# First route of a two-layer MoE block: rows turned by transposes and made by three engines in turn, the two experts of a token chosen batch by batch

## The reference, cut to what matters

```
h = _layernorm(x, axis=-1) * (1 + cb) + sb        # x: (4, 1024, 256); cb, sb: one row of 256 a batch
x = x + gb * _L0_ffn_ref(h, Wr, W1, W2, W3)

# in _L0_ffn_ref
xf = x.reshape(-1, C)                             # 4096 tokens of 256
gate_logits = xf @ Wr                             # 8 logits a token
w, idx = jax.lax.top_k(gate_logits, 2)            # the two best experts, the lower index where two are equal
w = jax.nn.softmax(w, axis=-1)
comb = jnp.sum(w[:, :, None] * jax.nn.one_hot(idx, NUM_EXPERTS), axis=1)
```

## Time and profile before

| what | value |
|---|---|
| median of 3 runs | 2876.08 us (2870.78 to 2876.3) |
| the profiled execution, its own time | 2874.07 us |
| its span in the profile | 2872.4 us |
| TensorE's mean granted clock in it | 0.935 of full speed |
| busy share: PE, DVE, ACT, POOL | 86%, 73%, 45%, 43% |

### The profile page before, as it was taken

One profiled execution on the slowest core, in us unless ns is written; L12 is line 12 of the kernel. 1 busy time (PEld: TensorE's weight loads), 2 busy tenths in 40 slices (PEclk: granted clock), 3 DMA queues, 4 the chain that ended last, 5 costly groups with the idle time before them and its releaser, 6 DMA issues.

```text
span 2872.4 us, 38064 instructions
## 1 busy us (share of the span) xinstructions
PE 2483.7 (86%) x12341; PEld 1788.6 (62%) x12342; DVE 2102.1 (73%) x4278; ACT 1296.7 (45%) x2564; POOL 1238.7 (43%) x532
## 2 busy tenths in 40 slices
PE   6677868768776759999699999999999999959998
PEld 4455545545555549999366666666666666747776
DVE  4999999999999756666666667766776667655554
ACT  4677677677675335554233324332433243311111
POOL 2799999999999226666100000020002000233344
PEclk8889989889987879999899999999999999969999
DMA  4645555555557254444400010001001000125554
GB/s 149 195 155 189 169 178 190 167 182 189 163 179 219 75 163 91 63 63 60 125 1 1 1 48 1 1 31 33 1 1 34 15 1 1 67 84 125 128 132 75
DMA packets 151375, 268.84 MB, mean 94 GB/s; under 512 B 18348, under 2 KB 107612, under 8 KB 150844
## 3 DMA queue, kind: packets, MB, share of 16 engines
q1 hardware_dynamic: 122460, 227.12, 25.1%
q0 software_dynamic: 28224, 37.78, 8.1%
q10 hardware_dynamic: 544, 2.10, 0.2%
HBM read 209.52 MB, written 57.43 MB: 93 GB/s over the span
## 4 chain that ended last, share of the span: by engine, by line
PE 45%; DVE 3%; issue 2%; ACT 1%; DMA 1%; POOL 0%; another core or an unknown queue 0%; SPq 0%; DVEq 0%; POOLq 0%
PE at_o_ps L2007 8%; PE at_s_ps L1983 8%; PE at_qk_ps L1965 6%; PE e_h_ps L1584 5%; PE e_y_ps L1595 5%; PE at_s_ps L2015 4%; PE at_pt_ps L1994 4%; PE at_qk_ps L1970 3%; PE at_s_ps L1965 1%; DVE at_small L2384 1%; PE e_x_ps L1573 1%; PE at_s_ps L1970 0%; ACT at_pt L2144 0%; PE at_qk_ps L1903 0%; ACT at_probs L2133 0%
## 5 line engine op out<-in xcount | busy, mean ns | idle before, releaser
L793 POOL TENSOR_TENSOR dbx<-u,b_all 128x2048 f32<-128x2048 f32 x128 | 578.8, 4536 | 71.3 <-DVE u L872 31.6
L1847 POOL DMA_INDIRECT slots<-at_r_rows,slot_of x64 | 64.5, 1008 | 1101.7 <-DVE slot_of L2300 1021.9
L676 ACT ACTIVATE da_ps<-delta,a_neg 128x512 f32<-128x512 f32 x512 | 347.9, 689 | 132.6 <-DVE hc L945 124.3
L2144 ACT COPY at_pt<-at_pt_ps 128x512 f32<-128x512 f32 (+3 forms) x384 | 171.6, 483 | 515.0 <-PE at_pt_ps L1994 508.8
L469 PE MATMUL y_ps<-ident,hc 128*128 128x128 f32 x1536 | 246.8, 306 | 81.9 <-DVE hc L945 81.3
L1983 PE MATMUL at_s_ps<-at_qk 128*128 128x512 f32 (+3 forms) x768 | 290.8, 488 | 0.0
L2007 PE MATMUL at_o_ps<-at_pt,at_v 128*128 128x512 f32 (+3 forms) x768 | 288.4, 487 | 0.0
L469 PEld LDWEIGHTS y_ps<-ident,hc 128*128 128x128 f32 x1536 | 201.6, 158 | 137.0 <-DVE hc L945 108.5
L2133 ACT ACTIVATE at_probs<-at_s_ps,at_small 128x128 f32<-128x128 f32 (+7 forms) x256 | 192.1, 751 | 169.8 <-DVE at_small L2386 166.6
L945 DVE TENSOR_TENSOR hc<-da_ps,c_all 128x512 f32<-128x512 f32 x384 | 256.9, 671 | 0.0
L935 DVE TENSOR_TENSOR_SCAN da_ps<-da_ps,state,dbx 128x512 f32<-128x512 f32 x192 | 242.9, 1274 | 4.5 <-ACT da_ps L676 3.6
(11 more groups left out here) (409 smaller groups left out, 5011.5 us busy)
## 6 DMA issues: line engine op xcount, KB each, us to landing
b_all<-bc_rows SPq DMA_DIRECT2D x128, 512.0 KB, 4.6
c_all<-bc_rows SPq DMA_DIRECT2D x128, 512.0 KB, 5.0
w_qkv<-L_ffn_w SPq DMA_DIRECT2D x32, 512.0 KB
slots<-zeros SPq DMA_DIRECT2D x40, 260.0 KB, 6.5
e_xs<-slots SPq DMA_DIRECT2D x16, 650.0 KB, 7.1
w<-L_ffn_W SPq DMA_DIRECT2D x24, 384.0 KB, 8.8
more<-zeros SPq DMA_DIRECT2D x16, 256.0 KB, 5.1
sums<-x SPq DMA_DIRECT2D x8, 512.0 KB, 7.0
```

The source lines that it names most:

```text
L676: nc.scalar.activation(da_ps[s % RING_DA][:], delta[:, c % 2, m, :], ACT.Exp, scale=sh.a_neg[:, m, n:n + 1]).then_inc(S["da_ready"], 1)
L793: nc.gpsimd.tensor_tensor(dbx[:, at % RING_DBX], pair, rows, ALU.mult).then_inc(S["dbx_ready"], 1)
```

## The change

The rows of a tile are made by three engines. Even tiles: DVE computes `half = (x - mean) * rstd` (a tensor_scalar). Odd tiles: ACT computes the same as `x * rstd + dif`, with `dif = -mean * rstd` made once by DVE. Then DVE multiplies by `mods1` (a tensor_tensor), and POOL adds `mods0` and writes the row (a tensor_tensor, 32 of them). The waits on `row_turned` and `rows_copied` go with POOL's step. On ACT one such `normalise` of the next group stands behind copy 1 and one behind copy 3 of each group. PE turns with `nc.tensor.transpose` in place of a matmul against the identity. The choice is made for each batch by itself, with the same 12 instructions on 64 numbers a partition: that of batch b-1 stands on DVE behind the rows of batch b, the last two behind all rows. `scale` of the last tile of a batch stands in the next batch's part, so behind the choice, save for the last batch. ACT no longer raises `score_ready`.

```diff
+            pool.wait_ge(sh.route_mods_in, 16)
+            for t in range(TILES):
+                b, j = t // TPB, t % TPB
+                pool.wait_ge(half_ready, t + 1)
+                pool.wait_ge(row_turned, t + 1)
+                if j % CT == 0:
+                    pool.wait_ge(rows_copied[j // CT], b * 16 + 1)
+                nc.gpsimd.tensor_tensor(row8[:, j, :], half[:, t % 4, :], sh.mods[:, 0, b, :], ALU.add).then_inc(row_ready, 1)
...
+            def normalise(t):
+                act.wait_ge(row_ready, t + 1)
+                nc.scalar.activation(half[:, t % 4, :], sh.x[:, t, :], ACT.Identity, bias=sh.dif[:, t:t + 1],
+                                     scale=sh.rstd[:, t:t + 1]).then_inc(odd_ready, 1)
+            act.wait_ge(norm_ready, 1)
+            for t in (1, 3):
+                normalise(t)
...
                     if g < GROUPS:
                         copy_turned(g * GT + i)
+                        if i % 2 and g < GROUPS - 1:
+                            normalise((g + 1) * GT + i)
...
-            act.wait_ge(logits_copied, B)
-            act.sem_inc(score_ready, 1)
...
-                    last = nc.tensor.matmul(turned[t % RT][:, k, :], row8[:, t % TPB, k * P:(k + 1) * P], sh.ident[:], start=True, stop=True)
+                    last = nc.tensor.transpose(turned[t % RT][:, k, :], row8[:, t % TPB, k * P:(k + 1) * P], sh.ident[:])
...
-            pe.wait_ge(masks_ready, 1)
+            pe.wait_ge(masks_ready, B)
...
-            norm_rows(nc, dve, sh, half, row8, half_ready, row_ready, row_free)
+            nc.vector.scalar_tensor_tensor(out=sh.dif[:], in0=sh.mean[:], scalar=-1.0, in1=sh.rstd[:],
+                                           op0=ALU.mult, op1=ALU.mult).then_inc(norm_ready, 1)
+            def normalise(t):
+                dve.wait_ge(row_ready, t + 1)
+                nc.vector.tensor_scalar(half[:, t % 4, :], sh.x[:, t, :], sh.mean[:, t:t + 1], sh.rstd[:, t:t + 1],
+                                        ALU.subtract, ALU.mult).then_inc(even_ready, 1)
+            def scale(t):
+                dve.wait_ge(odd_ready if t % 2 else even_ready, t // 2 + 1)
+                nc.vector.tensor_tensor(half[:, t % 4, :], half[:, t % 4, :], sh.mods[:, 1, t // TPB, :], ALU.mult).then_inc(half_ready, 1)
+            def halves(b):
+                for t in range(b * TPB, (b + 1) * TPB, 2):
+                    normalise(t)
+                    if t:
+                        scale(t - 1)
+                    scale(t)
+                if b == B - 1:
+                    scale(TILES - 1)
...
+            def choose(b):
+                at = slice(b * TPB, (b + 1) * TPB)
+                dve.wait_ge(logits_copied, b + 1)
+                ...
+            for b in range(B):
+                halves(b)
+                if b == 0:
+                    dve.wait_ge(consts_ready, 8)
+                else:
+                    choose(b - 1)
+            choose(B - 1)
+            dve.wait_ge(masks_ready, B)
```

More of the change, by code:

```diff
@@ L1047, in phase_route @@
         (gate_in, var_ready, std_ready, chain, half_ready, row_ready, row_turned, turn_copied, tall_done, tall_copied, logits_done,
-         logits_copied, consts_ready, score_ready, masks_ready, ranked, gap_ready, exp_ready, meta_ready, meta_stored, lane_hot, block_hot, block_set, second_set, map_done, map_copied, held_done,
+         logits_copied, consts_ready, norm_ready, even_ready, odd_ready, masks_ready, ranked, gap_ready, exp_ready, meta_ready, meta_stored, lane_hot, block_hot, block_set, second_set, map_done, map_copied, held_done,
          pool_chain) = (
             sem(n) for n in ("gate_in var_ready std_ready chain half_ready row_ready row_turned turn_copied tall_done tall_copied logits_done "
-                             "logits_copied consts_ready score_ready masks_ready ranked gap_ready exp_ready "
+                             "logits_copied consts_ready norm_ready even_ready odd_ready masks_ready ranked gap_ready exp_ready "
                              "meta_ready meta_stored lane_hot block_hot block_set second_set map_done map_copied held_done pool_chain").split())
@@ L1233, in _ @@
-            nc.vector.tensor_tensor(both[:], mask[:, 0], mask[:, 1], ALU.add).then_inc(masks_ready, 1)
+            nc.vector.scalar_tensor_tensor(out=sh.dif[:], in0=sh.mean[:], scalar=-1.0, in1=sh.rstd[:],
[4 more added lines that the diff above has]
+                                        ALU.subtract, ALU.mult).then_inc(even_ready, 1)
@@ new lines, in _ @@
+            over = lambda a: a.rearrange("p (t o) -> p t o", o=1).broadcast_to([P, TPB, NE])
+            def choose(b):
+                at = slice(b * TPB, (b + 1) * TPB)
+                dve.wait_ge(logits_copied, b + 1)
+                values, c = logits[:, at, :], cand[:, at, :]
+                for k in range(2):
+                    link(nc.vector.tensor_reduce(top[:, k, at], values, AX_X, ALU.max))
+                    link(nc.vector.tensor_tensor(c, values, over(top[:, k, at]), ALU.is_lt))
+                    link(nc.vector.scalar_tensor_tensor(out=c, in0=c, scalar=float(NE), in1=iota_e[:, at, :], op0=ALU.mult, op1=ALU.add))
+                    chosen = meta[:, at, 3] if k == 0 else idx[:, at]
+                    link(nc.vector.tensor_reduce(chosen, c, AX_X, ALU.min))
+                    link(nc.vector.tensor_tensor(mask[:, k, at, :], iota_e[:, at, :], over(chosen), ALU.is_equal))
+                    if k == 0:
+                        link(nc.vector.scalar_tensor_tensor(out=scores[:, at, :], in0=mask[:, 0, at, :], scalar=-3e38, in1=values, op0=ALU.mult, op1=ALU.add))
+                        values = scores[:, at, :]
+                nc.vector.tensor_tensor(both[:, at, :], mask[:, 0, at, :], mask[:, 1, at, :], ALU.add).then_inc(masks_ready, 1)
```

## The result

The changed kernel takes 2879.32 us, the median of 16 runs (2878.14 to 2882.89), against 2873.45 of the kernel before on the same chip (16 runs, 2870.78 to 2876.3). The ratio is 1.0019, with a 95% interval of 1.0012 to 1.0025: 5.5 us slower by the ratio, 5.9 by the medians. In the profiled executions the span grew from 2872.4 to 2878.7, but the Mamba phase ahead, which the change doesn't touch, was also 2.0 longer, and the phases behind, whose code is the same, about 2 shorter. So the phase is read by itself, from its first DVE instruction (line 95; 969.96 before, 971.95 after) to the end of the choice: 52.05 us before, 58.23 after.

The account below looks back on a forecast made before the run. A loop of waits over PE and ACT, 4.97 us a period, was taken to bound the phase; -1.2 + 4.6 + 0.7 + 1.6 - 2.4 = +3.3 us on the median of 2876.08 gives 2879.4, range 2872 to 2891.

Parts of the forecast that it names:

- one of its own signs of being wrong: On PE in the groups: the forecast is wrong if PEclk is 0.50 there.
- the period: PE and ACT loop: two shorter turns -0.60, normalise +0.50, so 4.97 becomes 4.87, 4.37 in the last group; -1.2 us.
- the clock: First product on PE: clock still at 0.50 after gapped turning, 3.4 long in place of 1.8; +1.6 us, bounds 0 and 3.2.
- the choice: On DVE: row 8b+7 waits behind choose(b-1), product at +7.2 not +4.87; 2.3 lost for b = 1 and 2, +4.6.
- the start: Rows 0 to 3 come 1.2 to 1.3 apart in place of 0.8; first product at about 979.2, +0.7 us.
- the tail: After the last product: the wait for logits stays 3.29, the last batch's choice is 3.0 in place of 5.46; -2.4 us.
- a rival with a chance of 0.17: PE's clock stays at 0.50 in the groups: 7.1 a period, +15.2, 2891.3 us; chance 0.17.
- Rows in step: DVE and POOL take turns: 2.47 a pair of tiles, 1.24 a row against the loop's 1.22; lead small, not gone.
- SP's queue: Weight loads start 13 to 14 us later; SP done at about 1054, DVE's last instruction at 1060.6, so hidden by 6 to 7.
- The POOL rival: POOL's add with its waits at 1.0, 2.9 a pair: rows set the pace at 5.8 a group; +9, 2885; chance 0.13.

Follow-up runs that it names:

- the new order: The changed kernel with ScalarE copying the product's result ahead of copy 1, so copy 1 and normalise leave the loop; 0.9996.
- the last version: Kernel before with first four tiles turned by matmuls, others by transposes, ScalarE copying the product first, choice by batch behind all rows; 2865.36 us, 0.9967.

## Why the prediction was right, and where it was not

The forecast was 2879.4 and within 0.2% as the likeliest; measured are 2879.32 and +5.5 us by the ratio against a predicted +3.3, at the very edge of that bound (by the medians, +5.9, just over it). That the two times agree to 0.1 us is luck: the forecast stood on a median of 3 runs, 2876.08, and with 16 runs the kernel before is at 2873.45. The direction came out, and the size within a factor of two. The account behind them did not, and one of its own signs of being wrong came true: PEclk was 0.50 for a part of six groups. Term by term, with the measured value in the stretch: the period -1.2 (-0.9), the clock +1.6 (+8.7), the choice +4.6 (+0.5), the start +0.7 (+0.3), the tail -2.4 (-2.5); predicted +3.3, measured together +6.1 of the stretch's +6.2. Two terms, off by +7 and -4, cancelled in part.

- **The period, -1.2.** Right as a price. At full clock the loop of transposes and normalise is 4.91 (6.54 less 1.63 of slow product, second period), predicted 4.87; the last period is 4.42, predicted 4.37. Transposes alone gave 4.42, normalise alone +0.49.
- **The clock, +1.6 for the first product.** This term is the one that was mis-sized. I took the slow clock for the first product alone, where it cost 1.34, and left the groups to a rival with a chance of 0.17. The products were longer than 1.88 by 1.34, 1.63, 1.56, 1.38, 1.09, 0.91, 0 and 0: 7.9 us; slow first turns in four periods add 0.8. The runs show the cause: halved turning holds the clock (periods of 4.42), ScalarE's instruction in the loop with matmuls holds it (5.46), both together lose it, in a kernel that has nothing else of the change. The rival was right in its mechanism and too dear (7.1 a period): the clock recovered in each product, or just behind it, so a period paid 1.2 to 1.6, not 2.2.
- **The choice in the stream, +4.6.** Right as a mechanism, hidden here. The row does wait behind the choice; in the open, at the full clock, it costs 1.6 (with matmuls, the slow turn taken off), 1.29 (6.75 against 5.46, the last tile scaled ahead) or 2.97 (6.86 against 3.89, in the loop with the new order), against 2.3 predicted. In the changed kernel the slow product runs meanwhile. The two periods were 6.64, of which 1.56 and 1.09 are the product's and 0.08 and 0.25 the slow turn's: only 0.1 and 0.4 remain above 4.91. And around five of the six such stalls of the three runs above the clock fell for the next product, which the working didn't have.
- **Rows in step.** Rows were dearer in the working than on the chip: 2.47 a pair by strict turn-taking, 1.93 measured, so 0.27 a row less. The turn-taking itself is there: the instruction that starts second is the longer one, the tensor_scalar 0.81 against 0.405, the tensor_tensor 0.94 against 0.42, POOL's add 0.84 against 0.71 to 0.77. But an instruction's recorded time overlaps the other engine's at its edges, by 0.25 where VectorE is first, so the full times don't add up. The Trainium skill's rule (SBUF — State Buffer, "Who interferes with whom") that a two-input instruction of VectorE and a reading one of GpSimd block each other fits all 8 tensor_tensors that started inside a POOL add. The instruction of the earlier trace rows has one input, so it bears on the tensor_scalar and not on this rule. The fear of late rows in general fell with the run of three engines' rows alone: there the periods are all alike.
- **The start, +0.7.** +0.3: POOL's first rows came closer together than I took it.
- **The tail, -2.4.** -2.5. The choice of the last batch took 3.04.
- **SP's queue.** (The prediction's 1060.6 adds 3.8 where its own sum says 3.3; nothing hangs on it.) The meta store was issued at 1043.5 (15.0 later than before, counted from each phase's start; predicted 13 to 14), SP waited 11.3 for it, and was done at about 1056 against DVE's last instruction at 1065.3. Hidden, as predicted, by 9 us.
- **The Trainium skill's rule on transposes** (TensorE: Matmul & The Clock Gate, "Part 4: PE-mode transpose"), by which the full clock doesn't engage for them, isn't what happened: with every tile turned twice by transposes the clock was 1.00 from the first product to the last, also where the same loop with half as many let it fall (in the groups, products of 1.88 against up to 3.50).
- **Two sums of the prediction.** The POOL rival's terms, 3.3 and 6.6, give +9.9, not +9: the 1.2 was taken off though it is counted already. And its chances of a slower kernel, 0.17, 0.13 and a sixth of 0.58, add up to 0.40, not 0.33.

What stays open: which of the gaps within a group decides over the clock, and why it holds in one group and falls in another of the same kernel (it held at the third product of the run with ScalarE's extra instruction, and at the first of the two equal stalls of the run with the last tile scaled ahead). The runs change the amount of work (each tile turned twice) or the length of the loop (ScalarE's instruction); no run moved the same work about within a period. And the whole kernel gained 10.6 us by the medians with the last version (9.5 by the ratio) where its stretch gained 11.1; the rest is within the interval.

## What to carry to other kernels

An instruction handed to an idle engine is free only if it doesn't stand in the queue ahead of one that a loop waits for: ScalarE was busy for 2 of every 5 us before, yet 0.5 us of its time in the loop of waits cost 0.5 us each time, and the order of two of its instructions was worth 0.63 a period (4.42 to 3.79), where the transposes were worth 0.55 (4.97 to 4.42). Work taken off TensorE shortens its part of the loop, but the same loop with less work and more waiting may lose the clock, so shorten the wait first and the work after. And work cut in pieces belongs where its engine has nothing left to do: in the stream of rows the pieces gave back 1.0 of their 2.4 us with a spare lead of rows, and 3.2 and more without one; behind the rows they held nobody up.

## What the runs showed of the hardware that was not expected

Useless work can keep the clock: with ScalarE's extra instruction in the loop, twice as many transposes kept the granted clock at 1.00 (2.4 GHz) in place of swinging between 0.50 and 1.00, and the profiled stretch was 4.5 us shorter (58.69 to 54.18); the timed difference of the two kernels, 0.0005, is within its noise. The clock can swing once a period for tens of microseconds: in the changed kernel it rose near the end of each slow product and fell again near the start of the next, five times in a row. With ScalarE's order changed, TensorE idled once for 2.80 us, ahead of a group's last turns, and the next product took 3.17 in place of 1.88. And VectorE and GpSimd beside each other don't cost the sum of their recorded times: a VectorE tensor_tensor that started 0.16 us ahead of a GpSimd add kept its 0.42, and the add took 0.84 in place of 0.71 to 0.77.
